# Causal attention in a fused transformer block: paired row maxima, the mask added by TensorE, and the products with v of two key blocks issued together

## The reference

```python
    x = x + 0.5 * _L0_ffn_ref(_layernorm(x, axis=-1), L0_ffn_W_fc, L0_ffn_W_proj)
    x = x + _L0_attn_ref(_layernorm(x, axis=-1), L0_attn_Wq, L0_attn_Wk, L0_attn_Wv, L0_attn_bv, L0_attn_Wo, L0_attn_bo)
    x = x + 0.5 * _L0_ffn_ref(_layernorm(x, axis=-1), L0_ffn_W_fc, L0_ffn_W_proj)
```

```python
        scores = jnp.einsum('bhsd,bhtd->bhst', q, k) * scale
        causal = jnp.triu(jnp.ones((S, S), dtype=bool), k=1)
        scores = jnp.where(causal, -jnp.inf, scores)
        probs = jax.nn.softmax(scores, axis=-1)
        out = jnp.einsum('bhst,bhtd->bhsd', probs, v)
```

## Time and profile before

| | us |
|---|---|
| Median of 3 runs | 1601.37 |
| The profiled execution | 1608.4, span 1606.7, mean granted TensorE clock 0.904 |
| First phase and the start of attention, to the first find | 0 to 409 |
| Lead-in of attention | 409 to 459 |
| Groups 0 to 6 | 459 to 1247 |
| Group 7 | 1247 to 1345 |
| Last phase | 1345 to 1607 |

### The profile page before, as it was taken

The page is one execution under the profiler, slowest core; times in us unless marked ns, Lnnn a source line. Parts: engine busy times, 40 slices in busy tenths (PEclk is TensorE's granted clock), DMA queues, the critical chain, the costliest instruction groups (busy, mean ns, idle before and its releaser), DMA issues. The chain is left out here.

```text
span 1606.7 us, 27137 instructions
## 1 busy us (share of the span) xinstructions
PE 1381.6 (86%) x8384; PEld 821.8 (51%) x8384; DVE 1139.5 (71%) x2689; ACT 860.6 (54%) x1155; POOL 229.9 (14%) x206
## 2 busy tenths in 40 slices
PE   5988888750799999999999989999999976899997
PEld 5877777640443343343343333433433422799986
DVE  5666676821788888877887887888888930567675
ACT  5644444310036666655665665666666655466564
POOL 0012222346001011010010110110110101110100
PEclk9999999875568899997997999999999978899999
DMA  5113333437152062070080260440620002222312
GB/s 204 40 40 105 105 118 100 150 123 95 13 69 34 6 83 24 5 101 8 9 98 5 30 82 5 55 52 6 72 34 5 8 8 68 92 80 92 95 51 66
DMA packets 101898, 97.86 MB, mean 61 GB/s; under 512 B 46288, under 2 KB 85200, under 8 KB 100048
## 3 DMA queue, kind: packets, MB, share of 16 engines
q1 hardware_dynamic: 101744, 95.98, 29.0%
HBM read 57.15 MB, written 37.75 MB: 59 GB/s over the span
## 5 line engine op out<-in xcount | busy, mean ns | idle before, releaser
L1001 ACT ACTIVATE probs<-s_ps 128x1024 f32<-128x1024 f32 (+3 forms) x640 | 542.7, 895 | 327.7 <-PE s_ps L1133 326.4
L1112 PE MATMUL m_ps<-kT,qT 64*128 64x512 f32 (+3 forms) x1280 | 478.9, 478 | 112.9 <-DMA qT<-qkT_parts 55.9
L1026 DVE TENSOR_REDUCE maxes<-m_ps 128x1 f32<-128x512 f32 x768 | 490.8, 684 | 48.5 <-PE m_ps L1112 44.2
L1112 PEld LDWEIGHTS m_ps<-kT,qT 64*128 64x128 f32 x1280 | 217.2, 201 | 502.2 <-DVE maxes L1026 274.0
L1133 PE MATMUL s_ps<-qT,kT 64*128 64x512 f32 (+3 forms) x1280 | 327.3, 416 | 13.8 <-DMA qT<-shiftT 10.5
L1031 DVE CUSTOM_DVE_ANT_0 masked<-m_ps,mask_b 128x384 f32<-128x384 f32 (+3 forms) x512 | 238.3, 488 | 130.6 <-PE m_ps L1112 125.0
L1150 PE MATMUL o_ps<-probs,v_w 128*32 128x512 f32 (+3 forms) x2560 | 322.4, 578 | 0.2 <-POOL probs L974 0.2
L974 POOL TENSOR_SCALAR_AFFINE_SELECT probs<-probs 128x512 f32<-128x512 f32 x128 | 81.6, 637 | 851.8 <-ACT probs L1001 851.8
L1133 PEld LDWEIGHTS s_ps<-qT,kT 64*128 64x128 f32 x1280 | 164.2, 198 | 41.0 <-ACT probs L1001 25.0
L313 ACT ACTIVATE relu_a<-ups_a 128x512 f32<-128x512 f32 x64 | 38.1, 596 | 100.8 <-PE ups_a L562 99.9
L1150 PEld LDWEIGHTS o_ps<-probs,v_w 128*32 128x32 f32 x2560 | 51.9, 111 | 76.5 <-issue 58.9
(11 more groups left out here) (124 smaller groups left out, 1917.7 us busy)
## 6 DMA issues: line engine op xcount, KB each, us to landing
kT<-qkT_parts SPq DMA_DIRECT2D x48, 256.0 KB
qT<-qkT_parts SPq DMA_DIRECT2D x96, 128.0 KB
qkT_parts<-qk_hi_a SPq DMA_DIRECT2D x32, 256.0 KB, 3.0
qkT_parts<-qk_lo_a SPq DMA_DIRECT2D x32, 256.0 KB, 3.4
qT<-shiftT SPq DMA_DIRECT2D x512, 1.0 KB
xin_a<-in_x SPq DMA_DIRECT2D x8, 512.0 KB, 4.0
xres_a<-in_x SPq DMA_DIRECT2D x8, 512.0 KB, 4.9
x<-xsum_a SPq DMA_DIRECT2D x8, 512.0 KB, 3.2
```

Of the source, the lines that this page charges most:

```text
L1001: act.activation(probs[:, b % PBUF, 2 * hp:2 * hp + 2, off:CH], s_ps[hp][:, :, off:CH], ACT.Exp, scale=D ** -0.5)\
L1026: dve.tensor_reduce(out, m_ps[:, bank, 0:width], AX.X, ALU.max).then_inc(max_read, 1)
L1112: pe.matmul(m_ps[:, bank, 0:width], qT[of % 2][r0:r0 + HR, j, h // 2, t * P:(t + 1) * P], kT[of % 2][r0:r0 + HR, h // 2, k * CH:k * CH + w ...
```

## The change

- `m_ps` becomes `MB` = 2 entries of two banks. A unit is now a pair of heads: 80 in a group (48 off the diagonal, 32 on it), two matmuls in the two row halves, one `max_done`, and one DVE reduction of 128x1024 (or narrower) to two columns.
- The mask is added on PE: on a diagonal unit two further matmuls of a bf16 identity with a bf16 mask, 128 columns each, accumulate onto it. The DVE operation with the mask and its read of the accumulator are gone.
- The negated maxima are turned by a PE transpose through the ring (`turn_shift`), placed three units after the step's last unit, and DVE copies them to `shiftT`. SP then issues 4 DMAs for a shift, not 16.
- `s_ps` becomes 3 banks of one head. Each score matmul waits for its own bank and each exponential is of one head (128x512): 1280, not 640.
- `products` is called only in odd slots g, for the blocks of slots g - 3 and g - 2 together. Units are dealt: the first after `scores(…, 0)`, the second after `scores(…, 1)`, the others after the products.
- SP issues the six loads (term m of q, then of k and v) in slots 0 to 5 of a group, each before that slot's stores and shifts.
- Everything is unrolled; the loop over pairs of groups and its register arithmetic are gone.

The core of the diff:

```diff
...
-        PAIRS = B * NG // 2
+        GROUPS = B * NG
...
         PBUF = 4
+        SB, MB = 3, 2
...
-        s_ps = [pb(f"s_ps{p}", [P, 2, CH]) for p in range(2)]
-        m_ps = pb("m_ps", [P, MB, CH])
+        s_ps = pb("s_ps", [P, SB, CH])
+        m_ps = pb("m_ps", [P, MB, 2, CH])
...
+        UNITS = [(j, t, hp, k, CH if k < j else P * (t + 1))
+                 for j in range(NJ) for t in range(T) for hp in range(G // 2) for k in range(j + 1)]
...
+                for j in range(NJ):
+                    last = max(i for i, (_, e) in enumerate(order) if e[0] == "unit" and e[1] == n and UNITS[e[2]][0] == j)
+                    after = [i for i, (_, e) in enumerate(order) if i > last and e[0] == "unit"][:3]
+                    at = after[-1] if after else last
+                    order.insert(at + 1, (order[at][0], ("shift", n, j)))
...
+        TERMS = [(m, x) for m in range(NT) for x in range(2)]
...
-                        for r in range(P // VW):
-                            c0 = VW * r + G * T * a + G * T // 2 * par
-                            sp.dma_start(out[:, :, r, :].bitcast(F32), shiftT[c0:c0 + G * T // 2, :]).then_inc(shift_in, 16)
...
+                        row, c0 = HR * par + KR + a, G * T * a + G * T // 2 * par
+                        out = qT[n % 2][row:row + 1, j, :, :].rearrange("o h (t q) -> o (h t) q", t=T)
+                        sp.dma_start(out.bitcast(F32), shiftT[c0:c0 + G * T // 2, :]).then_inc(shift_in, 16)
...
+                for x in range(BLOCKS):
+                    if x < len(TERMS) and n + 1 < GROUPS:
+                        if x == 0:
+                            wait(sp, s_done, G * block_no(n, 0, 0))
+                            wait(sp, v_ready, n)
+                        load(n + 1, *TERMS[x])
+                    moves(BLOCKS * n + x)
...
-                    act.wait_ge(pv_done, key_blocks(n, j, b) + 1)
-                    for hp in range(2):
-                        act.wait_ge(s_done, exp_units(n, j, b) + hp + 1)
-                        act.activation(probs[:, b % PBUF, 2 * hp:2 * hp + 2, off:CH], s_ps[hp][:, :, off:CH], ACT.Exp, scale=D ** -0.5)\
+                    blk = block_no(n, j, b)
+                    wait(act, pv_done, blk - PBUF + 1)
+                    for h in range(G):
+                        u = G * blk + h
+                        act.wait_ge(s_done, u + 1)
+                        act.activation(probs[:, b % PBUF, h, off:CH], s_ps[:, u % SB, off:CH], ACT.Exp, scale=D ** -0.5)\
                            .then_inc(exp_done, 1)
...
-                    dve.tensor_tensor_reduce(masked[:, u % 2, 0:width], m_ps[:, bank, 0:width], mask[:, CH - width:CH], 1.0, NEG,
-                                             ALU.add, ALU.max, out).then_inc(max_read, 1)
...
-            def negate(i, dn, j, k, found):
...
+                dve.tensor_reduce(maxes[:, j % 2, :, hp, t, k], m_ps[:, i % MB, :, 0:width], AX.X, ALU.max).then_inc(max_read, 1)
...
+                dve.tensor_copy(shiftT[:, :], m_ps[0:2 * G * T, i % MB, 0, 0:P]).then_inc(max_read, 1)
...
-                pe.matmul(m_ps[:, bank, 0:width], qT[of % 2][r0:r0 + HR, j, h // 2, t * P:(t + 1) * P],
-                          kT[of % 2][r0:r0 + HR, h // 2, k * CH:k * CH + width], start=True, stop=True)\
...
+                for par in range(2):
+                    r0 = HR * par
+                    mm = pe.matmul(m_ps[:, i % MB, par, 0:width], qT[n % 2][r0:r0 + HR, j, hp, t * P:(t + 1) * P],
+                                   kT[n % 2][r0:r0 + HR, hp, k * CH:k * CH + width], start=True, stop=True)
+                if k == j:
+                    for par in range(2):
+                        mm = pe.matmul(m_ps[:, i % MB, par, t * P:(t + 1) * P], identb[:, :], maskb[:, :],
+                                       start=False, stop=True, skip_group_check=True)
+                mm.then_inc(max_done, 1)
...
+                pe.transpose(m_ps[0:2 * G * T, i % MB, 0, 0:P], negparts[:, :, :].rearrange("p a c -> p (a c)"), ident[:, :])\
...
-                pe.wait_ge(exp_done, exp_units(n, j, b) + hp + 1)
-                for h in range(2):
-                    mm = pe.matmul(s_ps[hp][:, h, off:CH], kT[dn % 2][HR * h:HR * (h + 1), hp, b * P:(b + 1) * P],
-                                   qT[dn % 2][HR * h:HR * (h + 1), j, hp, off:CH], start=True, stop=True)
-                mm.then_inc(s_done, 1)
...
+                    u = G * block_no(n, j, b) + 2 * hp + par
+                    wait(pe, exp_done, u - SB + 1)
+                    r0 = HR * par
+                    pe.matmul(s_ps[:, u % SB, off:CH], kT[n % 2][r0:r0 + HR, hp, b * P:(b + 1) * P],
+                              qT[n % 2][r0:r0 + HR, j, hp, off:CH], start=True, stop=True).then_inc(s_done, 1)
...
-                    some(0)
-                    scores(i, dn, j, b, 0)
-                    some(1)
-                    scores(i, dn, j, b, 1)
-                    some(2)
-                    if b >= 2:
-                        products(i, dn, j, b - 2)
...
+                items = ITEMS.get(g, [])
+                scores(n, j, b, 0)
+                ring(items[:1])
+                scores(n, j, b, 1)
+                ring(items[1:2])
+                if g >= 2 and g % 2:
+                    products(*slots[g - 3])
+                    products(*slots[g - 2])
+                ring(items[2:])
...
```

More of the change, by code:

```diff
@@ L1184, in _, with ring @@
-            pe.wait_ge(const_in, 32)
-            for x in range(MAX_FROM, 0):
-                for u in unit_slots[x]:
-                    find(0, 0, x, 0, u)
-            steps(pe, body)
+            def ring(items):
+                for e in items:
+                    if e[0] == "unit":
+                        unit(e)
+                    elif e[0] == "shift":
+                        turn_shift(e)
+                    else:
+                        turn_sums(e)
+            pe.wait_ge(mask_ok, 2)
@@ new lines, in _ @@
+            for g in range(MAX_FROM, 0):
+                ring(ITEMS.get(g, []))
+            slots = [(n, j, b) for n, j in steps() for b in range(T * j + T)]
+            for g, (n, j, b) in enumerate(slots):
+                items = ITEMS.get(g, [])
[7 more added lines that the diff above has]
+                ring(items[2:])
@@ L1191, in build @@
+            for slot in slots[-2:]:
+                products(*slot)
+            ring(ITEMS[BLOCKS * GROUPS])
 def build(nc, x, w, out):
```

438 lines of the change are left out of this document (165 added, 273 removed).

## The result

| | before | after |
|---|---|---|
| Median, us | 1603.22 (1593.75 to 1606.89, 4 runs) | 1693.4 (1682.9 to 1699.59, 4 runs) |
| Ratio after / before, 95% interval | | 1.0565 (1.0491 to 1.064) |
| Profiled execution, span, us | 1606.7 | 1697.9 |
| To attention's first find | 409.4 | 403.6 |
| To attention's first exponential | 459.2 | 451.3 |

The change makes the kernel 5.7% slower. 1648 us was forecast, within 1570 to 1695. The sign came out; the size was half of what was measured (+90 us, and not +47), because time at half clock was put at nothing.

What follows compares the result with a forecast made beforehand. DVE's reductions were taken to set the pace before, the ACT and PE chain after. Groups 0 to 6 +45, group 7 +10, lead-in -7, loads -1.5: +46, span 1606.7 to 1653, forecast 1648 us, range 1570 to 1695.

Steps and rivals of the forecast that it cites:

- The chain: Attention through ACT and PE: two full slots without units take 5.55 us against 4.02, ACT running dry behind two product blocks.
- Lead-in and start: Before the groups: lead-in 7 us shorter, and 1.5 us saved because loads no longer wait for the mask's memset.
- DVE's relief: Reductions in each group: about 84 us of DVE work against 92, the 8 us spent on DVE's idle gaps.
- The rival in which DVE sets the pace: Full slots: DVE, not the chain, sets the time, 96 us a group and 1480 us in all; chance 0.12.
- The stall: Groups 0 to 6: store and shift queue behind six loads, stalling slot 7 or 12; 5 us a group, 35 in all.
- burst is hidden: Rival on the loads: stores and shifts land in time or wait where nothing is due, 1613 us; chance 0.26.
- The shift of step 2: Transfer behind all six loads: lands at about 35 us into a group, with slot 12 due at about 30.
- The sum for a group: Groups 0 to 6 without stalls: chain 99.6 us plus units, masks, sums, copies and slots 20 and 21, 114.0 against 112.6.
- Group 7: Last group: about 108 us against 98, +10, though rid of the 8 us wait for the shift.
- The mask: Mask matmuls on PE: ten diagonal pairs a group lie in the chain at 0.70 us each, 0.53 of it masks.
- the clock falls too: Rival: each stall in groups 0 to 6 brings a half-clock stretch, 25 to 45 us more, 1670 to 1695; chance 0.12.

Runs made afterwards that it cites:

- three variants: Kernel before with products grouped in odd slots, 1733.38 us; changed kernel with one block every slot, 1686.15; with loads spread, three heads queued, useless matmuls, 1628.57.
- a fourth: Changed kernel with DVE reducing half of each unit's columns and ACT exponentiating half of each head's columns: 1565.67 us, ratio 0.9697.
- the half-length reductions: Changed kernel with DVE reducing only the first half of each unit's columns: 1650.18 us, ratio 1.0232.
- either cure: Changed kernel with loads in slots 0, 1, 4, 5, 12, 13, 1653.22 us; or with two `att` buffers and loads left in the burst, 1653.68 us.
- the useless matmuls: Changed kernel with unread 64x512 score matmuls added in the last 20 slots, three pairs every two slots: 1676.12 us, ratio 1.0406.
- spread loads: Changed kernel with a group's six loads issued in slots 0, 1, 4, 5, 12 and 13, not 0 to 5: 1653.22 us, ratio 1.0262.

## Why the prediction was right in sign and short in size

**The chain: right where it stands alone.** Its period was forecast at 5.55 us, measured 5.47, and the same working gave three variants at full clock (4.9 and 4.87; 5.36 and 5.3; 5.2 and 5.22) and missed a fourth by 0.2 (4.4 and 4.6). ACT's idle time behind the products stood where it was placed. But the comparison with 4.02 us holds for slots without units only. With units, the six full pairs 16, 18 and 28 to 34 take 5.1 to 6.4 us at full clock in the kernel before, 5.7 in the mean, and 5.9 to 6.3 in the changed one, 6.1 in the mean: 0.4 us more a pair, not 1.5.

**Lead-in and start: right by luck.** -8.5 us was forecast and 459.2 to 451.3 is -7.9. But -7 of it was to be the lead-in and -1.5 the start, and the first find now stands at 403.56 and not at 409.38:

```profile
403.56 0.48 PE L995 MATMUL m_ps<-kT,qT 64*128 64x128 f32 x2 [52.31 <-DMA kT<-qkT_parts]
```

So the start gave 5.8 us and the lead-in 2.1 (49.8 to 47.7). DVE's work in it fell by some 4 us (45.8 to 41.5), but its idle time rose, and without the masks the lead-in takes 45.6: the forecast took DVE's gap to stay as it was.

**DVE's relief: right.** 84 us a group were forecast, 609 / 7 = 87 measured, and the forecast had said that it would be spent on gaps. The rival in which DVE sets the pace fell with the half-length reductions.

**The stall: right mechanism, and the half clock behind it left out.** The forecast was 5 us in seven groups, 35 us. The wait is 4.5 us in six, 27 us: group 0 has no store to wait behind. The half clock that follows makes it 40 us, which the forecast had split off as a rival (0.12) and not counted. The store of group 3 landed 24.7 us after the group's start, as the "some 24 us" had it. The rival *burst is hidden* is refuted: 40 us are bought back by either cure. The shift of step 2, the second of the two waits named, wasn't needed for it: more room for `att` alone was enough.

**The sum for a group: right at full clock, and compared with the wrong number. This is the step that failed.** 114.0 us was forecast without stalls, and 114.2 is what the pairs of slots add up to at full clock. (Luck has a part: slots 20 and 21 were given 6.5 us and take 7.4, others less.) But the forecast set this against a measured 112.6, which has half clock in it. The rows that showed it were at hand: the granted clock had a mean of 0.88 and 0.97 over two groups, and the kernel before spends 9.5 us in slots 20 and 21, at 0.63. Without these two, which never ran at full clock there, its group adds up to 99.4 us at full clock, and the changed kernel's to 106.8: 7.4 us more, not 1.4. And a changed kernel at full clock throughout never came: beside the stalls, groups 0 to 6 lose 28 us to half clock, in slots 20 and 21 (13 us), 24, 25, 32, 33, 36, 37 and a few early ones. Every pair of slots that is over 0.3 us longer than its full-clock time has a granted clock of 0.81 or less.

**Group 7: the same step.** 108 was forecast, 117.9 measured, 104.2 with the useless matmuls. "About 108, without units in its second half" took the period at full clock, which is 4 us more than group 7 takes at full clock, and put nothing for half clock, though the trace before had shown how the clock answers a wait. The wait for the shift did go.

**The mask: 0.39 and not 0.53 us each, but in more places.** Leaving it out gave 46 us, where the forecast had 10 x 0.53 x 7 = 37 us on the path and called the rest hidden. The two errors offset one another in part.

So the forecast span (1653) and the measured one (1697.9) are 45 us apart. Half clock makes 55: 28 in groups 0 to 6 beside the stalls, 13 behind the stalls, 14 in group 7. Everything else came out 10 lower: the waits by 8, group 7 at full clock by 4, with 1 more each in the groups' sums and ahead of them. The rival *the clock falls too* (1670 to 1695) gave the right range, but only in part for its reason: it named one stretch behind each stall, some 25 us, where 13 were measured, and nothing in the other slots of groups 0 to 6 or in group 7.

**What stays open.** The costs don't add: from the kernel before, grouping alone costs 8.2%; in the changed kernel, taking it out and putting the products between the scores buys 1.4% (spread loads, 1.0262 to 1.0122), with nothing gained at full clock in groups 0 to 6. What makes the 7.4 us a group at full clock wasn't taken apart: the masks are some of it, and shorter exponentials shorten it, but what sets 5.9 us for two full slots with units wasn't settled: not DVE's pace, and not only the heads queued in front of ACT. Why the same slots get full clock in one group and half in the next isn't shown either. No version of the changed kernel with all of its work beats the kernel before; the best leaves 1.2%.

## What to carry to other kernels

Ahead of a block of work that one engine does in one piece, count how much is queued for the engine behind it: with 1.5 us of exponentials in front of 2.3 us of products, ACT stood idle for 1.45 us each time, where the grouping was to save 0.3. A store that a buffer waits for must not stand behind a burst of loads; a second buffer and another place for the loads were equally good here (1654 and 1653 us). And a sum at full clock is compared with a sum at full clock: look in each stretch at the granted clock first, before taking a measured period as a price. Where a kernel has both clocks, ask what the new one will lose to the lower one; here that was the larger part of the error.

## What was not expected of the hardware

- Work that nobody needs made a kernel faster: 1693.4 to 1676.12 us, group 7 from 117.9 to 104.2 us, the granted clock of its worst stretch from 0.51 to 1.00. In the kernel before the same idea only moved the half clock on by two slots and cost 0.5%.
- One and the same slots of one kernel run at full clock in some groups and at about half in others: 7.4 and 10.1 us.
- A change from 64-row use of the array to a bf16 matmul on the whole array and back costs 0.39 us with two masks in it, of which the masks' starts are 66 ns apart.
- SP took 10.09 us to issue four transfers behind nine others, where 1.96 us were enough for four of the same later. Most of it is one issue: the tenth in a row takes 6.7 to 7.8 us in each of the six bursts of groups 1 to 6, where most others take 0.4 to 0.5. It holds up whatever is issued later. The kernel before shows the same in front of its lead-in, behind nine loads:

```profile
379.17 8.21 SPq L881 DMA_DIRECT2D kT<-qkT_parts  x1
```
